# A decoder of six layers on one core: turned maxima added to the queries, and three other regroupings

## The reference

```python
x = _layernorm(x + differential_attention(x))      # 32 query heads of 16, 8 key heads, causal
x = _layernorm(x + long_convolution(x, ctx))       # 32 groups of 8 channels
x = _layernorm(x + mixture_of_experts(x))          # the best 2 of 8 experts
x = _layernorm(x + attention(x))                   # "P" in the kernel: 16 heads of 32, causal
x = _layernorm(x + cross_attention(x, ctx))        # "C": one head of 512, keys ctx and x
x = _layernorm(x + shared_attention(x))            # "A"/"H": 16 query heads, one key head chosen by a gate, causal
```

```python
kv = vr[:, :, :, None, :] * x2r[:, :, None, :, :]
y = irfft(rfft(kv, n=fft_size) * k_f, n=fft_size)[..., :L]
out = jnp.einsum('bhijl,bhil->bhjl', y, x1r)
```

## Time and profile before

| | |
|---|---|
| median of 3 runs | 2247.85 us (2245.63 to 2248.08) |
| the profiled execution | 2249.93 us, its span 2248.1 us |
| TensorE busy | 2099.8 us, 93% of the span |
| VectorE busy | 1248.4 us, 56% |
| GpSimd busy | 546.9 us, 24% |
| ScalarE busy | 517.0 us, 23% |
| granted clock of TensorE, mean | 0.971 |

### The profile page before, as it was taken

How to read it: one execution, slowest core, us unless ns; L and a number is a source line. 1 busy time by engine, 2 the same in 40 slices (tenths; PEclk the granted TensorE clock), 3 DMA queues, 4 the chain that set the end, 5 groups by cost and what they waited for, 6 DMA issues and landing times. The chain is left out here.

```text
span 2248.1 us, 29336 instructions
## 1 busy us (share of the span) xinstructions
PE 2099.8 (93%) x11903; PEld 1226.3 (55%) x11903; DVE 1248.4 (56%) x1886; ACT 517.0 (23%) x783; POOL 546.9 (24%) x514
## 2 busy tenths in 40 slices
PE   6899999888999899899999879999999999999996
PEld 4444444333444466565565646566666666666653
DVE  2467777666999944022222234355757585847465
ACT  1444444440000121111111111222222222222221
POOL 2122222227777400011111310212221212111122
PEclk9999999989999999999999989999999999999997
DMA  9850000005111045412221520101010101010000
GB/s 175 98 41 29 29 29 20 31 19 193 41 41 48 28 145 213 171 66 66 66 66 60 202 76 29 48 1 48 1 57 1 57 1 38 1 29 10 1 10 20
DMA packets 65634, 129.58 MB, mean 58 GB/s; under 512 B 6400, under 2 KB 19840, under 8 KB 65504
## 3 DMA queue, kind: packets, MB, share of 16 engines
q1 hardware_dynamic: 44848, 75.39, 13.3%
q10 hardware_dynamic: 14976, 33.69, 4.1%
q0 software_dynamic: 5680, 18.62, 2.8%
HBM read 96.36 MB, written 41.81 MB: 61 GB/s over the span
## 5 line engine op out<-in xcount | busy, mean ns | idle before, releaser
L930 PE MATMUL conv_conv<-kv,toep 128*128 128x512 f32 x576 | 248.6, 594 | 0.0
L2267 DVE RECIPROCAL tail_inv<-tail_ring 128x256 f32<-128x256 f32 x64 | 112.4, 1757 | 179.8 <-PE tail_ring L1729 179.6
L1428 PE MATMUL moe_gu_ps<-gu,moe_xT 128*128 x624 | 199.8, 463 | 3.9 <-issue 2.3
L930 PEld LDWEIGHTS conv_conv<-kv,toep 128*128 128x128 f32 x576 | 108.7, 191 | 140.5 <-issue 124.4
L953 POOL TENSOR_TENSOR kv<-vT,cT 128x512 f32<-128x512 f32 x128 | 147.8, 1176 | 57.7 <-PE conv_conv L930 53.1
L1428 PEld LDWEIGHTS moe_gu_ps<-gu,moe_xT 128*128 128x128 f32 x624 | 116.4, 192 | 73.2 <-issue 24.2
L2012 POOL TENSOR_TENSOR tail_rstd_x<-tail_rstd_x,const_minus_half 128x2 f32<-128x2 f32 x32 | 22.6, 708 | 481.5 <-DVE tail_rstd_x L2219 481.5
L2019 POOL TENSOR_SCALAR_AFFINE_SELECT tail_expT<-tail_expT 128x1024 f32<-128x1024 f32 x64 | 71.2, 1113 | 276.0 <-ACT tail_expT L2089 275.3
L540 POOL TENSOR_SCALAR_AFFINE_SELECT front_expT<-front_expT 128x2048 f32<-128x2048 f32 x32 | 64.4, 2013 | 259.9 <-ACT front_expT L598 259.9
L1512 DVE TENSOR_TENSOR moe_hid<-moe_gu_ps,moe_silu 128x352 f32<-128x352 f32 x39 | 20.5, 525 | 180.0 <-PE moe_gu_ps L1428 180.0
L2089 ACT ACTIVATE tail_expT<-tail_scores 128x1536 f32<-128x1536 f32 x64 | 92.9, 1451 | 74.6 <-PE tail_scores L1707 74.6
(11 more groups left out here) (349 smaller groups left out, 3968.3 us busy)
## 6 DMA issues: line engine op xcount, KB each, us to landing
toep<-toeplitz SPq DMA_DIRECT2D x32, 320.0 KB, 2.9
y_slots<-moe_y ACTq DMA_DIRECT2D x39, 256.0 KB, 2.0
gu<-in_L_ffn_gate_up_proj SPq DMA_DIRECT2D x5, 1408.0 KB, 10.5
toeplitz<-filt_rows SPq DMA_DIRECT2D x1, 6144.0 KB, 67.1
front_e<-in_ctx SPq DMA_DIRECT2D x8, 512.0 KB, 5.9
toeplitz<-filt_rows SPq DMA_DIRECT2D x2, 2048.0 KB, 88.2
x_after<-x SPq DMA_DIRECT2D x8, 512.0 KB, 5.0
tail_x<-x_after SPq DMA_DIRECT2D x8, 512.0 KB, 3.7
```

Source lines behind the costliest of these rows:

```text
L930: ins = pe.matmul(bank, toep[p][:, mat * P:(mat + 1) * P], kv[p][:, c].rearrange("p b j i -> p (b j i)"), start=n == 0, stop=n == len(PART ...
L1428: ins = pe.matmul(gu_ps[:, s % 2, h, 0:HID], xT[:, c, :], wgu[c][:, e, h * HID:(h + 1) * HID], start=c == 0, stop=c == NC - 1)
L2267: link.after(dve.reciprocal(inv[c % 2][:], bank[:, S:2 * S]))
```

## The change

Four regions are changed.

1. **First stage.** The products with `pick` and ScalarE's copies to `shiftT` are gone. The splits of the maxima are placed in rows 16 to 17 of a strip for ab = 0 and 0 to 1 for ab = 1 (rows which the other head of the pair owns), and `shift(b, ab)` turns each half by itself: 16 products per batch in the place of 8. VectorE merges the turned rows with the queries (`apply_shift`: queries times the half mask, plus the turned rows), for ab = 0 into the new `q_first`, for ab = 1 into `qT` itself. It also adds ones to the two rows of the keys (L720). A turned unit is then four products in place of eight. In the first batch's round, `query(d, 1)`, `key(d)` and `query(d, 2)` are moved between the scores. `wo` is requested by ScalarE behind its first value copy. `mask_bf` is half as wide and read twice.
2. **Long convolution.** VectorE's steps of a group are made in pairs: two products, one sum of 1,024 elements; two additions, two products, one sum. The last group's second half is made tile by tile.
3. **Last stage, rounds 0 and 1** are written out by hand and merged: the projections of batch 1 stand among the steps of batch 0 (they lie in tiles which are free then, `q_of`, `k_of`, `v_of`), the cross attention of batch 0 among the steps of batch 1. `late_stored` is split in two.
4. **Last batch.** POOL's addition (L2022) is left out in its four units, and `weigh` reads three tiles with ones instead; residual, statistics, norm and store are made for each half by itself.

```diff
...
-                def shift(b):
+                def shift(b, ab):
                     pe.wait_ge(split_ready, b + 1)
                     for jp in range(2):
-                        bank = ring.claim(pe, ("M", b, jp))
+                        bank = ring.claim(pe, ("M", b, ab, jp))
...
                 def scoreT(b, n):
                     ab, kt, t = T_UNITS[n]
-                    if n == 0:
+                    if kt + t == 0:
                         for jp in range(2):
-                            drained(("M", b, jp))
+                            drained(("M", b, ab, jp))
                     bank = quads.claim(pe, ("T", b, n))
                     for g in range(4):
-                        pe.matmul(bank[:, g, :].rearrange("p (j q) -> p j q", j=4), pick[strip(g), ab],
-                                  shiftT[strip(g), :, t * P:(t + 1) * P], start=True, stop=False, skip_group_check=True)
-                    for g in range(4):
                         ins = pe.matmul(bank[:, g, :].rearrange("p (j q) -> p j q", j=4), kT[b % 2][strip(g), ab, kt * P:(kt + 1) * P],
-                                        qT[b % 2][strip(g), :, t * P:(t + 1) * P], start=False, stop=True, skip_group_check=True)
+                                        shifted(b, ab)[strip(g), :, t * P:(t + 1) * P], start=True, stop=True, skip_group_check=True)
...
-                        shift(a)
-                        if d is not None: query(d, 3)
                         if a == 0:
                             pe.wait_ge(made, 2)
-                            pe.wait_ge(pick_made, 9)
+                        shift(a, 0)
+                        if d is not None: query(d, 3)
                         scoreT(a, 0)
+                        shift(a, 1)
...
+                def apply_shift(b, ab):
+                    for jp in range(2):
+                        key = ("M", b, ab, jp)
+                        bank = filled(key).rearrange("p (j s) -> p j s", s=S)
+                        dve.scalar_tensor_tensor(out=shifted(b, ab)[:, 2 * jp:2 * jp + 2, :], in0=qT[b % 2][:, 2 * jp:2 * jp + 2, :],
+                                                 scalar=half[:, ab:ab + 1], in1=bank, op0=ALU.mult,
+                                                 op1=ALU.add).then_inc(ring.drained_sem(key), 1)
...
                         for t in range(NT):
                             invert(f, 1, t)
                             if a is None: scale_half(f, 1, t)
+                            elif t == 0: apply_shift(a, 0)
                         if a is not None: scale_heads(f, 1)
+                    elif a is not None:
+                        apply_shift(a, 0)
+                    if a is not None: apply_shift(a, 1)
...
+                    weighted(h, 0)
+                    weighted(h, 1)
+                    taken(h, 1)
+                    sums(h, 0, 2)
+                    taken(h, "both")
+                    if h < H - 1:
+                        completed(h, 2)
+                        completed(h, 3)
+                        taken(h, 3)
+                        for lc in (2, 3):
+                            ins = dve.tensor_tensor(total[:, lc - 2], total[:, lc - 2], context_of(lc, h, 2), ALU.mult)
+                        link.after(ins)
+                        sums(h, 2, 2)
...
+                cross_rows(0, 1)
+                dve.wait_ge(ring.drained_sem(("C", "w", 0, 1)), ring.count(("C", "w", 0, 1)))
+                norm("x3", 2)
+                statistics("x5", 0)
+                mix("P", 1, 3)
+                add_plain(1)
...
-                    if 0 <= a < B:
+                    if 0 <= a < B - 1:
                         sp.wait_ge(normed["x6"], a + 1)
                         sp.dma_start(out_rows[a], buf("x6", a)[:]).then_inc(stored[a % 3], 16)
+                for t in range(NT):
+                    sp.wait_ge(normed["x6"], B + t)
+                    sp.dma_start(out_rows[B - 1][:, t], buf("x6", B - 1)[:, t]).then_inc(last_stored, 16)
...
```

## The result

The changed kernel takes 2236.52 us (median of 7 runs, 2232.71 to 2239.28) against 2248.53 us for the kernel before (7 runs, 2245.63 to 2254.34): ratio 0.9944, 95% interval 0.9931 to 0.9957. It is 12 us faster. In experiments that were run once, the time says little, since the runs of the changed kernel alone spread over 6.6 us; there the reading rests on stretches of the trace. 2223 us was forecast, with a range from 2212 to 2234, so the sign was right and the size about half. The profiled execution took 2239.28 us with a span of 2237.4, 10.7 us less than the span of before. The two traces divide these 10.7 us as follows; each limit is the start of the same instruction on TensorE in both.

What follows compares the result with a forecast made beforehand. TensorE, busy 93 to 97% in the first stage's rounds and the convolution, was taken as the bound. Terms -1.2 - 5.2 + 0.2 + 5.3 - 5.2 - 17 - 2 = -25.1 us gave 2223 us, range 2212 to 2234.

Steps and rivals of the forecast that it cites:

- Start: Start of first stage: wv lands 2.3 us earlier, ScalarE's four issues add 1.2; net -1.2 us, between +1.2 and -3.
- First batch: First stage, a = 0: moved queries and key fill gaps, shift earlier, clock gap filled; -5.2 us, between -1.5 and -7.
- Middle rounds: First stage, batches 1 to 6: removed products pay back a 1.0 us wait and second shift; +0.2 us, -5 to +7.
- Rival A: Middle rounds: combining steps reading PSUM cost 1.5 us each, the wait is 2.5 a round; +8, 2231 us; chance 0.08.
- Last batch: First stage, a = 7: reciprocals before the first combining step delay the first turned unit 6.5 us; +5.3, between +2 and +7.
- Convolution: Long convolution: paired VectorE steps, 0.61 us each without waiting, let VectorE catch up with TensorE; -5.2 us, -3 to -8.
- rival D: Long convolution: back-to-back products hold POOL longer; 0.3 us a head beyond its spare time gives +9, 2232 us; chance 0.03.
- Merged rounds: First two rounds of last stage: 156.2 us fall to 138 to 139, floor 122 plus 16; -17 us, -10 to -21.
- the 2 us of half clock: Merged rounds: half clock counted behind the wait for mix 3, within the 16 us above the floor.
- rival B: Merged rounds: the merged prologue gives half, as short waits come every 4 us; +8, 2231 us; chance 0.09.
- The sign of being wrong: Wrong if middle rounds differ from 56 us by over 1 us, or the merged rounds last over 146.
- End and the rest: Last batch of last stage: POOL's addition removed -1.5, norm and store in halves -0.5; -2 us, between 0 and -3.

Runs made afterwards that it cites:

- experiment 6: Changed kernel with query(d, 3) ahead of the shift instead of behind it in the first stage's first batch: 2236.31 us (one run).
- experiment 7: Changed kernel with GpSimd's four gathers of batch 3 put behind batch 1's four causal masks in the merged rounds: 2235.55 us (one run).
- experiment 10: Changed kernel with mix 3 of batch 1 ahead of x3's norm and x5's statistics on VectorE: 2234.09 us (one run).
- experiment 8: Changed kernel with the moves of experiments 1, 6, 7 and 10, last-batch reciprocals in VectorE's gaps, x4's norm ahead of batch 1's first maxima: 2215.55 us, ratio 0.9860.
- experiment 9: Changed kernel with the last stage of the kernel before: 2253.07 us (10 runs), ratio to before 1.0013.
- experiment 11: Kernel of experiment 8 with batch 1's last weighting ahead of cross attention's second output half and mix 3 ahead of cross_rows: 2210.61 us, ratio to before 0.9825.
- experiment 1: Changed kernel with VectorE's first-half merge moved ahead of the reciprocals of the batch before, in the first stage: 2229.38 us (4 runs), ratio to before 0.9900.

## Why the prediction was wrong, point by point

**Start.** Right in kind. The wait for wv fell from 6.78 to 1.51 us, by 5.3 and not by 2.3. The 1.2 us for ScalarE's four issues did not come: from the value product to the first score unit it took 15.04 us at full clock (experiment 6) and 15.28 before. In some executions half clock gave part back. -2.5 in the profile, -5.5 in others.

**First batch: the step that failed is "the gap that let the clock fall is then filled".** The chain came out as forecast: the shift was put near 55 and stood at 53.93, 26.5 us behind the first score unit instead of 29.7. But the two queries that were moved had covered the last reduction and the split. Up to the shift the clock was 0.98 (before: 0.83), so the gaps in the chain were filled as forecast. But without the two queries TensorE idled 3.35 us in front of the shift, and the clock fell there: from the shift to the end of the batch it was 0.78 (before: 0.86), and this part took 28.26 us instead of 25.19. What the chain gained was lost at half clock. The prediction had a price for this, -1.5 if the clock falls anyway, and even that was better than the -0.1 measured. Experiment 6 showed further that covering this gap only moves the half clock: in a stretch where TensorE is busy 43 of 55 us, the time went with the clock (50.6 or 54.5 us) more than with the order. What makes the clock fall in one execution and not in the next stays open.

**Middle rounds: the term that was mis-sized is the removal.** The wait of 1.0 us in front of the first turned unit was forecast at 1.0 and measured at 1.00, in all six rounds. The second shift cost 0.46 (forecast 0.44). The removed products gave 6 x 0.10 to 0.12 = 0.6 to 0.7 us a round, where I had taken the distance of two starts, 0.23, as the price of a group. The sum 1.0 + 0.46 - 0.6 to 0.7 = 0.8 to 0.9 us is the measured one, (227.08 - 223.56) / 4 = 0.88. My sentence that the wait is paid back unit by unit falls with it. Over six rounds that is 5.3 us; the table has 3.7, since the first of these rounds, from shift to shift, took 57.54 us before, 1.65 more than the others, and 56.44 after. Rival A, dearer merges, is not what happened: the two took 1.41 us.

**Last batch.** Right: 8.3 us were forecast from the split to the first unit, the trace has 8.0, and the stretch cost +6.1 against +5.3.

**Convolution: the step that failed is the estimate of 0.61 us for a step of a pair.** It holds for the pairs that read PSUM (1.28 for two). The pair of two SBUF operands takes 2.79 us instead of 1.29 (and 2.38 before, unpaired), and VectorE stays in step with GpSimd, about 5 us behind TensorE, instead of catching up. The prediction cited the rule and took the consequence for GpSimd (rival D) and not for VectorE. GpSimd's busy time in the stage did not change (187.0 us in both).

**Merged rounds: the step that failed is the 2 us of half clock.** This is the largest miss, 8.0 us. The sum of the waits was near: of the 16 us forecast above the floor 14 were idle time, and the window has 147.2 - 131.8 = 15.4. Their composition was off: GpSimd's gathers in front of the first mask (3.30 us) were not in the sum, though the change moves the masks past them. The granted clock is 0.94, so 0.12 of the stretch ran at half speed: 8.8 us lost if TensorE has work all that time, where 2 were counted. TensorE is busy for 131.8 us where the floor had 122. The fall stood behind three waits, of 2.30, 3.30 and 4.67 us; experiments 7 and 10 each took one away and gained 3.7 us, 0.8 and 1.7 of it beyond the wait itself. With all three shortened the clock was 0.99 and the rounds 136.4 us, near the forecast. So rival B (chance 0.09), in which the merged rounds give half, came true in its size; its reason, short waits every 4 us, is not what the trace shows. The sign of being wrong that the prediction named, merged rounds over 146 us, came too; the middle rounds stayed within their 1 us.

**End and the rest.** The last batch gave 2.6 us (forecast 2.0). The other 2.8 us at the hand-written rounds and 1.5 in the middle stage are half clock that the profiled execution of the kernel before had and this one has not; no edit stands behind them. The middle stage, the same in all these kernels, took 503.0 to 503.3 us in experiments 7 to 11 and 505.9 in experiment 1. So 4.3 of the 10.7 us between the two traces are luck.

**The range.** It reached to 2234 and the median is 2236.5. Four terms missed by 3 to 8 us each, all in the direction of less gain: the merged rounds (8.0) and the first batch (5.1) through the clock, the middle rounds (3.5) through the price of the removed products, the convolution (3.3) through the pair beside GpSimd. The better start and the luck hid 6 us of this. The clock I had put near its best value in both places.

## What to carry to other kernels

Before work is moved into a gap, look at what it covered where it stood; the uncovered wait is a cost of the move. A small group of products in front of a larger one was worth the change in the distance of the groups behind it here, 0.10 us, and not the 0.23 by which it started ahead: measure it by a run without the group. A step that the matrix engine waits for belongs ahead of everything that nobody waits for yet: one step moved on VectorE let the next stage start 9.2 us earlier here (ratio to before 0.9900 instead of 0.9944), and with the other repairs the kernel takes 2208 to 2215 us instead of 2236.5.

## What the runs showed of the hardware

- Half clock added to the cost of waits here: behind a wait of 2.30 us the turn of 1.04 took 1.97 and the product group of 3.70 after it 5.65, behind 3.30 us the weighting of 0.86 took 1.51, but behind 2.65 us an output product stayed at full clock (7.10) where behind 2.61 and 2.06 it did not (8.80). The length of the wait alone does not tell.
- The same order in the same stretch took 54.45 us three times and 50.64 once, with granted clocks of 0.84 and 0.93.
- Two VectorE products of 512 elements back to back took 2.79 us with both operands in SBUF beside GpSimd, 1.29 with GpSimd done, and 1.28 beside GpSimd with one operand in PSUM.
- One indirect gather held GpSimd for 0.96 to 1.02 us; with four in a row ahead of a mask TensorE waited 3.30 us for it, with the gathers behind the masks 0.42.
